# Moving 42 pieces of the two absolute weight sums from the attention groups into the first three projection blocks of a transformer layer

## The chip, the cores and the metric

The kernel runs on all eight cores of one Trainium2 chip. Each core takes one batch element (2048 tokens of width 2048) and reads the same weights; there is no exchange between cores. The metric is the device time in microseconds of the slowest core. The program names the engines PE (TensorE, matmul), DVE (VectorE), ACT (ScalarE), POOL (GpSimd) and SP (SyncE, which here only issues transfers). Each engine takes its instructions strictly in the order written and stops at the first one whose wait isn't met.

## The reference

One layer in two halves, each with a layer norm ahead and a residual add behind:

```
h   = layernorm(x)
q,k,v = h @ W* + h @ A* @ B*            # 16 query heads, 4 key/value heads of 128, rank 16
q,k = rmsnorm, rotary on 64 of 128, q *= gain
y   = causal softmax(q k^T / sqrt(128)) @ v
y  -= (y . v/|v|) v/|v|                 # component along the token's own value removed
x   = x + y @ Wproj + y @ p_A @ p_B
h   = layernorm(x)
s_w = mean(|W|) + 1e-8;  W_q = clip(round(W / s_w), -1, 1) * s_w    # for W_up, W_gate, W_down
x   = x + (silu(h @ W_up^T) * (h @ W_gate^T)) @ W_down^T
```

W_up and W_gate have 8192 x 2048 elements each. A mean of absolute values over all of W_up and one over all of W_gate must be known before the first panel of either is rounded to -1, 0 or 1. This case is about where those two sums are computed. They are the only reason for which the first half of the kernel reads W_up and W_gate at all.

## The kernel before

**Front.** The tokens are 16 row tiles of 128. A first stage (0 to about 173 us) normalises and transposes them into `slabA` and does query, key and value of head group 0. Then `attention` walks four groups, one per key/value head, of 136 score steps each (`PER`; a step is one query tile against one key tile for four heads). A step issues one score matmul (L769), an exponential on ACT (L781), up to two products with the values (L797, four matmuls each), and in the first three groups a share of the next group's query, key and value matmuls (L396, 512 in a group, from step 8 on). DVE and ACT also carry the norms and evictions of those tiles (L436 to L517 on DVE, L416 to L450 on ACT), and POOL the rotary part and two of the steps that finish an output tile. The order is written out by the loop itself: short queues of closures with due steps (`for_act`, `for_dve`, `for_bank`), no scheduler. The program holds attention twice, with and without a shift of the scores, and branches on the size of the gains; all gains are one, so the version without runs. At the start of the fourth group POOL issues sixteen loads that bring Wproj into `slabA`.

**The pieces.** `pieces` cuts W_up and W_gate into 256 pieces of 128 x 1024 float32 (512 KB). `abs_load` has SP load the next piece into one of three places (`pw`), once the place is free; `abs_sum` waits for the piece, sums its absolute values into one column of `pacc` on ACT (L199) or DVE (L202), and at once asks for the next load into the place that came free. So three pieces at most are under way. 13 are summed in the first stage. In the groups the loop keeps a target, `ABS_A` (222) pieces by the end of the third group and 256 by the end of the fourth, and issues a sum when it is behind: one on ACT when ACT has nothing due and the lag is over 1, and one on DVE when DVE has nothing due or the lag is over 3. Steps 0 to 9 of the first three groups issue none. That gives 69, 69 and 70 pieces in the first three groups and 35 in the fourth, 162 of the 256 on DVE.

**Projection.** Four blocks of 512 tokens. A block first multiplies the block's attention output `yts[s % 2]` (2 MB, read back from memory by `load_y`) with the rank-16 matrix (`lowrank_y`, L1154), which is the first thing in a block to need that operand, and then with 16 slices of Wproj (`proj_mm`, L1170 and L1175). `proj_post` adds each slice to the residual on DVE (L1186), squares it on ACT (L1196), and accumulates sum and sum of squares on POOL (L1205, L1208). After three slices of the next block come the statistics and the normalisation of the block (`stats`, `apply`) into `slabB`. The two buffers `yts` take turns: the operand of block s + 1 is loaded at the start of block s, when block s - 1 has been read. `finish_scale` turns the columns of `pacc` into the two scales; it makes DVE wait for everything that ACT has been given so far, and stands behind slice 8 of block 0. The scales are first used in block 3.

**FFN.** 192 panels of up, gate and down, bounded by PE, to the end. Nothing of it is touched.

Of the kernel before, what the change touches and what calls it, by code (L numbers as in the profile page):

```python
# [99 lines left out]
def build_program():  # L100
# [31 lines left out]
    with ExitStack() as outer:  # L132
# [5 lines left out]
        def emit(general):  # L138
# [5 lines left out]
                        "xs0", "xs1", "pw0", "pw1", "pw2", "gns", "ys0", "ys1",  # L144
# [34 lines left out]
            piece_next = [0]  # L179
# [3 lines left out]
            def abs_load(s, slots, sems, frees):  # L183

                n = piece_next[0]
                if n >= len(pieces):
                    return
                piece_next[0] += 1
                mi, src, col = pieces[n]
                wait("sync", frees[s])  # L190
                ld = dma("sync", sems[s], slots[s], src)
                pend.append((slots[s], col, ld, s))
# [419 lines left out]
            pw_args = (pw, ("pw0", "pw1", "pw2"), pw_free)  # L612
            ABS_0 = NT - 3
# [59 lines left out]
            ABS_A = 222  # L673
# [6 lines left out]
            def attention(general):  # L680
# [306 lines left out]
                while n < NPAIR or n_av < NPAIR:  # L987
# [37 lines left out]
                    if n < NPAIR and not (r < 10 and g < HKV - 1):  # L1025

                        lag = (ABS_0 + n * (ABS_A - ABS_0) // (3 * PER) if g < HKV - 1 else
                               ABS_A + (r + 1) * (256 - ABS_A) // PER) - n_abs
# [26 lines left out]
                assert not for_act and not for_pool and piece_next[0] == 256  # L1055
# [95 lines left out]
            def lowrank_y(s):  # L1151
                wait("tensor", pab, yl_tok[s], ya_bank_free[0], front_bank[0])
                for k in range(ND):
                    tp = op("tensor", lambda e, k=k: e.matmul(  # L1154
                        bank(0)[0:48, :], pa[:, k, :], yts[s % 2][:, k, :],
                        start=(k == 0), stop=(k == ND - 1)), inc=(k == ND - 1))
                wait("scalar", tp, blk_end[s - 1] if s else None)
                ya_tok[0] = ya_bank_free[0] = op("scalar", lambda e: e.activation(
                    ya, bank(0)[0:48, :], AF.Copy))
# [265 lines left out]
            load_y(1)  # L1425
            early = []
            for s in range(NB):
                if 1 <= s < NB - 1:
                    load_y(s + 1)
                lowrank_y(s)  # L1430
                if s == 0:
# [11 lines left out]
                    for i in range(5):  # L1443
                        proj_post(s, i)
                else:
# [21 lines left out]
                    proj_post(s, 5)  # L1467
                for i in range(5 if s == 0 else 6, ND):
                    proj_mm(s, i)
                    proj_post(s, i)  # L1470
                    if s == 0 and i == 8:
# [141 lines left out]
```

How the kernel before makes its waits and increments, by code:

```python
    def wait(self, eng, *tokens):  # L46
        for tok in tokens:
            if tok is None:
                continue
            sem, tgt = tok
            assert 0 < tgt <= self.cnt[sem]
            if self.met.get((eng, sem), 0) >= tgt:
                continue
            self.met[eng, sem] = tgt
            h = self.h[sem]
            self.ops[eng].append(lambda e, h=h, tgt=tgt: e.wait_ge(h, tgt))
# [1 line left out]
    def op(self, eng, fn, sem=None, inc=True):  # L58
        if not inc:
            self.ops[eng].append(fn)
            return None
        sem = sem or MAIN[eng]
        h = self.h[sem]
        self.cnt[sem] += 1
        self.ops[eng].append(lambda e, fn=fn, h=h: fn(e).then_inc(h, 1))
        return sem, self.cnt[sem]
# [1474 lines left out]
            def body(e):  # L1541
                for f in fast[eng][:f0[eng]]:
                    f(e)
                if eng in ("tensor", "vector"):
                    e.wait_ge(sems["dv"], flag_set[1])
                    large = e.value_load(flag)
                    with e.If(large == 1):
                        for f in full[eng][g0[eng]:g1[eng]]:
                            f(e)
                    with e.Else():
                        for f in fast[eng][f0[eng]:f1[eng]]:
                            f(e)
                else:
                    for f in fast[eng][f0[eng]:f1[eng]]:
                        f(e)
                for f in fast[eng][f1[eng]:]:
                    f(e)
```

## Time and profile before

| | us |
|---|---|
| Median of three runs (lowest 3891.25, highest 4554.52) | 3892.86 |
| The profiled execution | 3895.69 |
| Its span on the slowest core, core 7 (the cores: 3872.2 to 3894.1) | 3894.1 |
| First stage, to the first steps of attention | about 0 to 173 |
| Attention group 1, 2, 3 (borders by the loads that POOL issues at their starts) | 186 to 382, 382 to 581, 581 to 780 |
| Attention group 4 | 780 to 918 |
| Projection | 918 to about 1230 |
| FFN | about 1230 to 3894 |
| Busy over the span: PE, DVE, ACT, POOL | 3694.9 (95%), 1773.2 (46%), 930.3 (24%), 687.7 (18%) |

The table is read together with the stretches. The shares over the span are dominated by the FFN, in which PE is busy all the time, so 95% says little about the first 1230 us. In the groups PE is at nine tenths, DVE and ACT at two thirds, and the mean busy share of the 16 DMA engines at seven to eight tenths. Matmul ends are modelled, so PE's busy time is an upper value.

### The profile page before, as it was taken

The page shows a single profiled execution, that of the slowest core. Times are in us where ns is not written, and L with a number is a line of the kernel's source. Part 1 is how long each engine was busy: PE and PEld are TensorE (multiplying, and loading weights), DVE is VectorE, ACT ScalarE, POOL GpSimd, SP SyncE. Part 2 cuts the span into 40 slices and gives each one's busy share as a digit, 9 for nine tenths or more (in the row PEclk, how much of TensorE's full clock was granted, in tenths as well). Part 3 has the DMA queues.
Part 4 walks back from the last instruction along what each step waited for, and adds up shares of the span by engine and source line. Part 5 has one row for each costly group of instructions (what it writes and reads, how often), then busy time and mean ns, then how long its engine had stood idle before and what let it go on. Part 6 is the DMA issues. An engine that isn't in the chain of part 4 may idle for free.

```text
span 3894.1 us, 52465 instructions; the slowest of 8 cores (3872.2 to 3894.1 us)
## 1 busy us (share of the span) xinstructions
PE 3694.9 (95%) x19512; PEld 1787.0 (46%) x19512; DVE 1773.2 (46%) x2309; ACT 930.3 (24%) x1662; POOL 687.7 (18%) x835
## 2 busy tenths in 40 slices
PE   6898898958998999999999999999999999999999
PEld 4555555534333444444444444444444444444444
DVE  5666676644346333344433334433333443333443
ACT  4566676754111544200000100000100000101000
POOL 3355555445534000000000000000000000000000
PEclk9999999979999999999999999999999999999999
DMA  6577777696334877546422225632222663222364
GB/s 170 159 217 207 204 218 202 200 206 216 126 116 143 302 276 256 191 177 230 173 76 76 76 76 206 227 141 76 76 76 76 230 230 114 78 76 79 110 229 155
DMA packets 123949, 629.65 MB, mean 162 GB/s; under 512 B 13120, under 2 KB 13440, under 8 KB 73008
## 3 DMA queue, kind: packets, MB, share of 16 engines
q1 hardware_dynamic: 96960, 469.80, 35.6%
q0 software_dynamic: 26736, 156.45, 13.1%
q8 instruction: 163, 2.67, 0.3%
q14 instruction: 90, 0.74, 0.1%
HBM read 555.55 MB, written 92.27 MB: 166 GB/s over the span
## 4 chain that ended last, share of the span: by engine, by line
PE 82%; DMA 7%; DVE 5%; issue 3%; POOL 2%; ACT 1%; DVEq 0%; SPq 0%; POOLq 0%; ACTq 0%
PE accps L1366 67%; PE gps L396 5%; PE accps L1170 4%; DMA pw<-W_gate 3%; PE yps L797 2%; PE sps L769 1%; DMA pw<-W_up 1%; DMA yst<-xb 1%; DMA bm0t<-v_B 1%; DVE pacc L202 1%; DVE slabB L1249 1%; POOL xreg L1208 1%; PE gps L401 1%; DVE ss L436 1%; DMA bm1t<-v_B 0%
## 5 line engine op out<-in xcount | busy, mean ns | idle before, releaser
L1366 PE MATMUL accps<-slabB,xreg 128*128 128x512 bf16 x8192 | 1773.5, 380 | 4.4 <-DVE slabB L1249 4.4
L1366 PEld LDWEIGHTS accps<-slabB,xreg 128*128 128x128 bf16 x8192 | 802.4, 98 | 975.0 <-issue 11.7
L1366 PE MATMUL accps<-slabA,xreg 128*128 128x512 bf16 x4096 | 884.7, 380 | 0.0
L1379 ACT ACTIVATE xreg<-accps,scl 128x512 f32<-128x512 f32 x256 | 175.1, 687 | 2052.4 <-PE accps L1366 2052.4
L1366 PEld LDWEIGHTS accps<-slabA,xreg 128*128 128x128 bf16 x4096 | 400.7, 98 | 483.3
L1334 DVE TENSOR_SCALAR xreg<-xreg,scl 128x2048 bf16<-128x2048 f32 x192 | 247.3, 1288 | 601.9 <-PE accps L1366 577.6
L1337 DVE SCALAR_TENSOR_TENSOR xreg<-xreg,scl 128x2048 bf16<-128x2048 f32 x192 | 453.1, 2360 | 20.4 <-DVE xreg L1334 0.5
L396 PE MATMUL gps<-wq,slabA 128*128 128x512 bf16 (+1 forms) x2048 | 416.9, 335 | 14.8 <-DMA wq<-Wqkv 12.0
L1393 DVE SCALAR_TENSOR_TENSOR xreg<-accps,scl,xreg 128x512 f32<-128x512 f32 x256 | 192.0, 750 | 471.3 <-PE accps L1366 471.3
L1383 DVE TENSOR_TENSOR slabA<-xreg,accps 128x512 bf16<-128x512 f32 x256 | 175.2, 686 | 503.6 <-PE accps L1366 500.4
L781 ACT ACTIVATE pring<-sps 128x512 bf16<-128x512 f32 x510 | 297.7, 610 | 148.6 <-PE sps L769 116.7
L72 POOL DMA_DIRECT2D acc_scr<-xreg x48 | 35.5, 739 | 1558.4 <-DVE xreg L1393 1558.4
L396 PEld LDWEIGHTS gps<-wq,slabA 128*128 128x128 bf16 x2048 | 195.2, 100 | 142.2 <-issue 38.8
L202 DVE TENSOR_REDUCE pacc<-pw 128x1 f32<-128x1024 f32 x162 | 194.3, 1213 | 136.2 <-DMA pw<-W_gate 72.2
L1170 PE MATMUL accps<-xreg,slabA 128*128 128x512 bf16 x1024 | 238.0, 387 | 12.0 <-DVE xreg L1186 8.1
L769 PE MATMUL sps<-qT,kT 128*128 128x512 bf16 x510 | 202.8, 400 | 10.7 <-DVE mq L460 5.6
L1170 PEld LDWEIGHTS accps<-xreg,slabA 128*128 128x128 bf16 x1024 | 97.0, 99 | 138.0 <-issue 35.6
L1420 ACT ACTIVATE xreg<-xreg 128x2048 f32<-128x2048 f32 x64 | 121.8, 1905 | 70.0 <-DMA xreg<-W_down 70.0
L72 POOL DMA_DIRECT2D outT<-xreg x16 | 11.0, 685 | 641.4 <-DVE xreg L1393 641.4
L797 PE MATMUL yps<-v1b,pring 128*128 128x129 bf16 x884 | 88.3, 233 | 32.8 <-DVE t1a L824 23.7
L797 PE MATMUL yps<-v1a,pring 128*128 128x129 bf16 x1088 | 100.9, 227 | 14.6 <-DVE t1b L824 7.4
L797 PEld LDWEIGHTS yps<-v1a,pring 128*128 128x128 bf16 x1088 | 80.0, 101 | 55.2 <-issue 22.9
(165 smaller groups left out, 2165.9 us busy)
## 6 DMA issues: line engine op xcount, KB each, us to landing
xreg<-W_down SPq DMA_DIRECT2D x128, 1024.0 KB, 7.8
pw<-W_up SPq DMA_DIRECT2D x128, 512.0 KB, 5.7
pw<-W_gate SPq DMA_DIRECT2D x128, 512.0 KB, 5.7
xreg<-W_up SPq DMA_DIRECT2D x64, 1024.0 KB, 5.1
xreg<-W_gate SPq DMA_DIRECT2D x64, 1024.0 KB, 5.0
xreg<-acc_scr POOLq DMA_DIRECT2D x64, 1024.0 KB, 7.5
acc_scr<-xreg POOLq DMA_DIRECT2D x48, 1024.0 KB, 5.2
outT<-xreg POOLq DMA_DIRECT2D x16, 1024.0 KB, 5.2
```

The costliest lines, as they stand in the source:

```text
L202: frees[s] = op("vector", lambda e: e.tensor_reduce(pacc[:, col:col + 1], buf, AX.X, ALU.add, apply_absolute_value=True))
L396: op("tensor", lambda e, out=out, dt=dt, w=w, lo=lo, hi=hi: e.matmul(out, slabA[:, dt, ts], w[:, dt % 2, lo:hi], start=(dt == 0), stop=Fal ...
L769: s_tok[n] = op("tensor", lambda e: e.matmul(bank, kT[g % 2][:, kt * 128:(kt + 1) * 128], qT[:, qt, :], start=not general and not first, s ...
L781: a = op("scalar", lambda e: e.activation(p, rbank(bank_of[n]), AF.Exp))
L797: tp = op("tensor", lambda e, h=h: e.matmul(Yv[y][:, h // 2, h % 2, :], p[:, h * 128:(h + 1) * 128], v1[g % 2][:, kt, :], start=first and ...
L1170: op("tensor", lambda e, k=k: e.matmul(bk, wpj[:, i, k, :], yts[s % 2][:, k, :], start=(k == 0), stop=False), inc=False)
L1334: m = op("vector", lambda e: e.tensor_scalar(t, src, scl[:, 8 + mi:9 + mi], None, ALU.is_lt))
L1337: quant_tok[k] = op("vector", lambda e: e.scalar_tensor_tensor(t, src, scl[:, 4 + mi:5 + mi], t, ALU.is_gt, ALU.subtract))
L1366: pan_tok[k][tc] = op("tensor", lambda e, tc=tc, dt=dt, mov=mov: e.matmul(bank(st_ + tc), tern[s][:, dt * 128:(dt + 1) * 128], mov, start= ...
L1379: evict[k][tc] = op("scalar", lambda e, tc=tc, cs=cs: e.activation(silu[:, cs], bank(st_ + tc), AF.Silu, scale=scl[:, 1:2]))
L1383: evict[k][tc] = op("vector", lambda e, tc=tc, cs=cs: e.tensor_tensor(hid[:, j, cs], silu[:, cs], bank(st_ + tc), ALU.mult))
L1393: e.scalar_tensor_tensor(accs[a][:, ds], bank(st_ + tc), scl[:, 12:13], accs[a][:, ds], ALU.mult, ALU.add))
```

## The change

Forty-two pieces are no longer summed in attention. The targets become `ABS_A` = 174 and `ABS_F` = 214, so the groups take 53, 53, 54 and 41 pieces where they took 69, 69, 70 and 35: sixteen fewer in each of the first three, six more in the fourth. The other 42 are summed in blocks 0, 1 and 2 of the projection, 14 in each, all on ACT (`block_pieces`). Their four places lie in the buffer `yts[(s + 1) % 2]`, where the next block's operand will stand. Therefore the load of that operand is issued only behind slice 10 of the block, and waits there for the last of the 14 sums. The first four piece loads of block 0 follow the loads of the residual; those of blocks 1 and 2 follow the load of the next block's residual. `finish_scale` moves from slice 8 of block 0 to slice 14 of block 2.

```diff
-                        "xs0", "xs1", "pw0", "pw1", "pw2", "gns", "ys0", "ys1",
+                        "xs0", "xs1", "pw0", "pw1", "pw2", "gns", "pw3", "ys0", "ys1",
...
-                if n >= len(pieces):
+                if n >= piece_end[0]:
                     return
...
+            ABS_A, ABS_F = 174, 214
+            piece_end[0] = ABS_F
...
-            ABS_A = 222
...
                         lag = (ABS_0 + n * (ABS_A - ABS_0) // (3 * PER) if g < HKV - 1 else
-                               ABS_A + (r + 1) * (256 - ABS_A) // PER) - n_abs
+                               ABS_A + (r + 1) * (ABS_F - ABS_A) // PER) - n_abs
...
             load_x(0, 0)
-            load_y(1)
+            def piece_args(s):
+                return ([xf(16 * ((s + 1) % 2) + 4 * i, 1024) for i in range(4)],
+                        ("pw0", "pw1", "pw2", "pw3"), piece_free)
+
+            piece_free = [None] * 4
+
+            def block_pieces(s, i):
+                args = piece_args(s)
+                if i == 0:
+                    piece_end[0] = ABS_F + 14 * (s + 1)
+                    piece_free[:] = [blk_end[s - 1]] * 4 if s else [None] * 4
+                    if s == 0:
+                        wait("sync", *front_early)
+                    for k in range(4):
+                        abs_load(k, *args)
+                for _ in range(2):
+                    if i >= 2 and pend:
+                        abs_sum("scalar", *args)
+                if i == 10:
+                    assert not pend
+                    wait("sync", *piece_free)
+                    load_y(s + 1)
...
             for s in range(NB):
-                if 1 <= s < NB - 1:
-                    load_y(s + 1)
                 lowrank_y(s)
...
                     for i in range(5):
                         proj_post(s, i)
+                        block_pieces(s, i)
...
                     proj_post(s, 4)
                     proj_post(s, 5)
+                    if s < NB - 1:
+                        for i in range(6):
+                            block_pieces(s, i)
                 for i in range(5 if s == 0 else 6, ND):
                     proj_mm(s, i)
                     proj_post(s, i)
-                    if s == 0 and i == 8:
+                    if s < NB - 1:
+                        block_pieces(s, i)
+                    if s == NB - 2 and i == 14:
                         up_s = finish_scale(1, 64, 128, bank(0))
                         gate_s = finish_scale(2, 192, 128, bank(0))
```

Two places in the order of instructions show the change. The first is ACT in the second attention group, from one square of the queries (L416) to the next; `pring<-sps` are the exponentials, `pw,pacc<-pw` is the sum of a piece. Before:

```order
L416 ACTIVATE sq<-gps 128x512
L781 ACTIVATE pring<-sps 128x512 x2
L426 ACTIVATE sq<-gps 128x256
L429 ACTIVATE vf<-gps 128x128
L781 ACTIVATE pring<-sps 128x512 x2
L447 ACTIVATE lss<-ss,epsc 128x5
L450 ACTIVATE lss<-lss 128x5
L781 ACTIVATE pring<-sps 128x512
L199 ACTIVATE pw,pacc<-pw 128x1024
L781 ACTIVATE pring<-sps 128x512 x3
```

The same stretch of ACT in the changed kernel:

```order
L416 ACTIVATE sq<-gps 128x512
L782 ACTIVATE pring<-sps 128x512 x2
L426 ACTIVATE sq<-gps 128x256
L429 ACTIVATE vf<-gps 128x128
L782 ACTIVATE pring<-sps 128x512 x2
L447 ACTIVATE lss<-ss,epsc 128x5
L450 ACTIVATE lss<-lss 128x5
L782 ACTIVATE pring<-sps 128x512 x4
```

The piece between the exponentials is gone, and nothing else has moved. The second place is SP's queue in block 1 of the projection, from the residual loads of block 1 (`xT`) on; `acc_scr` are the stores of the new residual, `y_scr` is the next block's operand. Before, where the operand's load stands ahead of all of them:

```order
L72 DMA xreg<-y_scr 128x8192 [waits pe]
L72 DMA xreg<-xT 128x4x512 [waits dv,xo0,ac,po]
L72 DMA xreg<-xT 128x4x512 [waits dv,xo1,ac,po]
L72 DMA xreg<-xT 128x4x512 [waits dv,xo2,ac,po]
L72 DMA acc_scr<-slabB 128x4x512 [waits dv]
L72 DMA xreg<-xT 128x4x512 [waits dv,xo3,ac,po]
L72 DMA acc_scr<-xreg 128x4x512 [waits dv] x3
```

And in the changed kernel:

```order
L72 DMA xreg<-xT 128x4x512 [waits dv,xo0,po]
L72 DMA xreg<-xT 128x4x512 [waits dv,xo1,po]
L72 DMA xreg<-xT 128x4x512 [waits dv,xo2,ac,po]
L72 DMA acc_scr<-slabB 128x4x512 [waits dv]
L72 DMA xreg<-xT 128x4x512 [waits dv,xo3,ac,po]
L72 DMA xreg<-W_gate 128x1024 [waits pe]
L72 DMA xreg<-W_gate 128x1024 x3
L72 DMA xreg<-W_gate 128x1024 [waits ac] x10
L72 DMA acc_scr<-xreg 128x4x512 [waits dv]
L72 DMA xreg<-y_scr 128x8192 [waits ac]
```

The operand's load now stands behind fourteen piece loads, ten of which wait for a sum on ACT, and behind one store.

## Rows read from the trace of the kernel before

**Rows 1.** busy time by window, core 7: groups one, two and four (columns in the first line)

```profile
core 7: us, PE busy (x) PEld busy (x) DVE busy (x) ACT busy (x) POOL busy (x), PEclk, DMA share, GB/s
186.00:382.00 196.00, 177.02 (x1377) 106.97 (x1376) 132.40 (x259) 131.79 (x280) 102.70 (x131) 0.95 0.76 213
382.00:581.00 199.00, 176.04 (x1383) 107.50 (x1382) 136.98 (x267) 133.33 (x286) 109.05 (x140) 0.96 0.77 210
780.00:918.00 138.00, 87.48 (x803) 59.79 (x800) 78.19 (x113) 81.22 (x160) 68.87 (x71) 0.80 0.90 225
```

**Rows 2.** waits of the first, second and third group: us in total, times, longest

```profile
DVE pacc L202 <- DMA pw<-W_up: 38.0, 16, 6.4
...
DVE pacc L202 <- DMA pw<-W_up: 25.6, 13, 5.0
...
DVE pacc L202 <- DMA pw<-W_gate: 28.0, 16, 3.3
```

**Rows 3.** instructions on tile pw, whole span: count, ns min/median/max, first and last start

```profile
L202 DVE TENSOR_REDUCE pacc<-pw x162: 1202/1212/1221, 196.8 to 916.4; 128x1 f32<-128x1024 f32 x162
L199 ACT ACTIVATE pw<-pw x94: 1046/1050/1078, 80.1 to 785.7; 128x1024 f32<-128x1024 f32 x94
...
DMA to landing us min/median/max: 3.6/5.7/20.0
```

**Rows 4.** timeline, second group: start us, us, engine, line, what, idle before and releaser

```profile
456.46 1.22 DVE L202 TENSOR_REDUCE pacc<-pw 128x1 f32<-128x1024 f32 x1 [5.03 <-DMA pw<-W_up]
...
462.58 1.05 ACT L199 ACTIVATE pw<-pw 128x1024 f32<-128x1024 f32 x1
...
463.10 0.62 PE L797 MATMUL yps<-v1b,pring 128*128 128x129 bf16 x8 [1.28 <-DVE t1a L824]
```

**Rows 5.** windows of 20 us, instructions of L396 (query, key, value matmuls) alone

```profile
486.00:506.00 20.00, 13.06 (x66) 6.00 (x65) 1.00 0.81 217
586.00:606.00 20.00, 6.39 (x29) 2.83 (x29) 0.91 0.76 170
```

**Rows 6.** last group in two parts, instructions of L202 alone

```profile
780.00:861.00 81.00, 14.86 (x13) 0.72 1.01 213
861.00:918.00 57.00, 26.56 (x22) 0.92 0.76 242
```

**Rows 7.** DMA issues in the same two parts: count, KB each, median us to landing

```profile
pw<-W_gate SPq DMA_DIRECT2D x14, 512.0 KB, 12.5
...
pw<-W_gate SPq DMA_DIRECT2D x19, 512.0 KB, 5.8
```

**Rows 8.** DMA in 1030 to 1045, in 40 slices of 1039 to 1068, in 1060 to 1080

```profile
DMA packets 2096, 4.18 MB, mean 278 GB/s; under 512 B 57, under 2 KB 57, under 8 KB 2096
...
GB/s 407 410 412 387 322 342 302 376 395 407 249 164 62 37 25 0 0 0 0 0 263 407 410 364 3 0 0 0 0 0 0 0 0 0 11 0 0 0 0 0
...
xreg<-y_scr SPq DMA_DIRECT2D x1, 2048.0 KB, 9.2
```

**Rows 9.** timeline of projection block 1

```profile
1039.36 0.37 SPq L72 DMA_DIRECT2D xreg<-xT  x1
...
1045.17 0.63 ACT L1196 ACTIVATE xreg<-xreg 128x512 f32<-128x512 f32 x1 [2.00 <-POOL xreg L1208]
...
1064.55 0.63 ACT L1196 ACTIVATE xreg<-xreg 128x512 f32<-128x512 f32 x1 [2.93 <-DVE xreg L1186]
...
1067.40 3.63 PE L1154 MATMUL accps<-xreg,pa 128*48 128x512 bf16 x16
```

**Rows 10.** timeline of projection block 0

```profile
945.04 3.55 SPq L72 DMA_DIRECT2D xreg<-xT  x3
...
962.66 0.35 PE L1260 MATMUL accps<-tots,ones_f 128*128 128x1 f32 x2 [3.11 <-DVE tots L1257]
964.56 6.28 PE L1170 MATMUL accps<-xreg,slabA 128*128 128x512 bf16 x16
...
994.34 3.63 PE L1154 MATMUL accps<-xreg,pa 128*48 128x512 bf16 x16
```

More of the change, by code:

```diff
@@ L178, in emit @@
                       for k in range(64) for h in range(2)]
-            piece_next = [0]
+            piece_next, piece_end = [0], [0]
             pend = []
@@ L1054, in attention @@
                     abs_sum("vector", *pw_args)
-                assert not for_act and not for_pool and piece_next[0] == 256
+                assert not for_act and not for_pool and piece_next[0] == ABS_F
                 while next_slot:
@@ L1151, in lowrank_y @@
             def lowrank_y(s):
-                wait("tensor", pab, yl_tok[s], ya_bank_free[0], front_bank[0])
+                wait("tensor", pab, yl_tok[s], *ya_bank_free, front_bank[0])
                 for k in range(ND):
```

## The prediction

> **What bounds the kernel now.** I read the busy time by stretch first. In the first and second group PE is busy for 177 of 196 us and for 176 of 199 us, at a mean granted clock of 0.95 and 0.96; DVE and ACT are busy for two thirds [rows 1]. So PE has some 20 us of holes in a group and loses some more to the lower of its two clock levels after them. In the fourth group it is busy for 87 of 138 us, and the DMA engines at 0.90 [rows 1]. Next the waits. DVE, which takes its work in order, stands before a piece sum for its DMA 16, 13 and 16 times in the three groups, for 38.0, 25.6 and 28.0 us [rows 2]. The timeline shows what that does: DVE stands 5.03 us until 456.46, its late work ends late, and PE stands at 463.10 for 1.28 us, released by a DVE instruction behind the sum [rows 4]. Stepping through the three groups in this way, nearly every hole of PE outside the first 15 us of a group follows a piece wait within 7 us.
>
> Why pieces are late is arithmetic. A load lands in a median of 5.7 us, a sum on DVE takes 1.21 us [rows 3], and there are three places: a place turns over in about 7 us. A score step takes 1.44 us (196 us / 136). Where the third piece after a given one comes fewer than five steps later, it has to be waited for. Counting through the loop's order, that is so 64 times in the first three groups.
>
> **Change, part 1: sixteen pieces fewer in each of three groups.** The same count in the changed order gives 14 instead of 64. What a group could take: where nothing is held up, 66 of the L396 matmuls pass in 20 us [rows 5]; 512 in a group make 155 us, and the eight steps without them some 7, so 162. The group takes 196 to 199, so 35 us are lost. About half of that is lost at the group's start, where short output tiles follow each other and only 29 matmuls pass in 20 us [rows 5] with few pieces there; removing pieces hardly changes that. The other 18 us I put on the piece waits: about 12 of standing and 6 of lower clock. With 78% (50 of 64) of the causes gone, 14 us a group, **-42 us** in all. The removed sums themselves (1.21 us on DVE, 1.05 on ACT [rows 3]) lie beside PE's work and I count nothing more for them. Bounds: at least -20, if only half of the standing goes and the clock does not recover; at most -60, if the starts improve too. I take a value near the middle since rows 4 ties the standing to the pieces directly.
>
> **Part 2: six pieces more in the last group.** It falls in two. Until 861 us the DMA engines are full (1.01) with Wproj and 13 pieces [rows 6]; two more pieces of 0.52 MB at 213 GB/s are 5 us. After it, 22 pieces pass in 57 us [rows 6], one in 2.6; landing takes 5.8 us [rows 7], and three places allow one in (5.8 + 1.2)/3 = 2.3 us, so this part is already nearly as fast as its three places let it be. Four more are 4 x 1.2 (DVE only) to 4 x 2.6 us; I take 7. Together **+12**, between 0 (ACT and DMA absorb all) and +20. In the first part a piece takes 12.5 us to land [rows 7]; if a further piece costs a whole turn of its place, 12.5/3 = 4.2 us, two cost 8 instead of 5, and part 2 becomes +15. The Trainium skill, "DMA: Bandwidth & Descriptors", section "Queues, rings and completion order", says that a DMA engine serves the queues that have work in turn, packet by packet; by that rule three places on SP's queue against sixteen Wproj loads on POOL's get a fixed share and the +15 holds. The trace (12.5 us against 5.8) leans that way; it moves the sum by 3 us and I leave it at the bytes.
>
> **Part 3: the next operand arrives late.** This is where the change costs. Block 1: the residual load of block 2 is issued at 1039.36, and the low-rank matmuls of block 2, which need the operand, start at 1067.40, directly behind the last slice [rows 9]. In these 28 us now come, in one chain, that load (1 MB), 14 pieces (7.3 MB), the last sum, then a store (1 MB) and the operand (2.1 MB). The engines moved 278 GB/s over 15 busy us and 302 to 412 in single slices of 0.7 us [rows 8]. At 350 GB/s a piece takes 1.5 us: the residual has landed at about 1044.4, the fourteenth piece at 1065.4, its sum ends at 1066.7, and the operand, 9.2 us from issue to landing [rows 8], lands at 1076. PE stands **8 to 9 us**, and the sixteen matmuls behind a stand take longer: after the holes at 962 to 964 us they took 6.28 us [rows 10], against 3.63 in the even run of rows 9. I add 2 us for the clock, so +11.
>
> Block 0: the residual loads start at 945.04 [rows 10], four of 1 MB; the pieces come behind them, the first at about 960.5, the last, with a store between, at 983; sum, operand at 993.5. The low-rank matmuls of block 1 began at 994.34 [rows 10]. Without `finish_scale` at slice 8, which held PE for 3.1 us at 962.66 and about 1.1 behind it and cost 2.6 in clock [rows 10], they could begin 7 us sooner; the operand takes that back, and with its own clock loss block 0 is at **+1**.
>
> Block 2: `finish_scale` stands behind slice 14, and its wait is for all of ACT. In block 1, eight pieces on ACT stand ahead of the square of slice 6 and six more ahead of that of slice 9. ACT is held by the pieces until about 1066.7, and from there the squares follow POOL at 2.63 us each (0.63 busy and 2.00 of waiting [rows 9]). The square of slice 14, at 1064.55 now [rows 9], comes at about 1077. In block 2's time that is a stand of 13 us for PE, then 2 to 3 for the two small reductions, then slice 15 (3.9 us); the operand has long landed. The low-rank matmuls of block 3 begin 16 us late, with the clock **+18**.
>
> Projection: 1 + 11 + 18 = **+30**. Bounds: at 400 GB/s it is -2 + 8 + 14 = +20, at 278 GB/s +9 + 19 + 23 = +51; if PE did not wait at all it would be -7. I take 350, which lies between the mean over 15 us and the slices.
>
> **Sum.** -42 + 12 + 30 = 0 against the profiled execution of 3895.7 us, which lies 2.8 above the median of the runs, 3892.9. I add 2 us for parts that I may have counted at nothing, and forecast **3895 us**; each time below is 3892.9 + 2 and the sum of its case. It is no change that a measurement of this kernel can tell. It can tell about 2%, that is 78 us.
>
> **Rivals.** *The projection takes the pieces for nothing.* For it: of the 40 slices of rows 8 more than half are at or near 0 GB/s, so the engines have room. Against it: 11.4 MB in 28 us, less the fixed part of two landings and a sum, needs well over the 412 GB/s of the best slice [rows 8]. Then -42 + 12 - 7 = -37, **3858 us**; chance 0.18.
>
> *The groups don't speed up: another wait takes the pieces' place.* The holes of PE end at DVE or POOL work, and DVE keeps two thirds of its load; POOL is busy for 103 to 109 of 196 us [rows 1] and its chain of three steps for an output tile sets the pace at a group's start. If it does elsewhere too, a group gains 5 us: -15 + 12 + 30 = +27, **3922 us**, slower than before. It decides if PE's holes stay at 15 us or more in a group while the piece waits fall below 10. For it: the 29 matmuls in 20 us [rows 5]. Against it: the stretch of 66 between. Chance 0.18.
>
> *Memory is slower with all cores in the projection reading pieces*, at 278 GB/s: -42 + 12 + 51 = +21, 3916 us; chance 0.14.
>
> *The groups gain all they can* (-60) at the forecast's projection: 3877 us; chance 0.12. The forecast itself has 0.35 within some 10 us; 0.03 is left for what I have not seen.
>
> **The numbers.** The range takes in all of these: from 3858 up, a little further down where the first and fourth would add up in part, gives low 3858; the two slow cases with some overlap give high 3928. Faster by over 2% would need -78 us, more than the groups' whole loss outside their starts: 0.01. Slower by over 2% needs the highest bound of each term at once: 0.02. Same: 0.97.
>
> **What would show it.** In the changed profile: groups one to three of 182 to 186 us, with DVE's wait for pieces under 10 us each; group four of about 150 us; PE standing before the low-rank matmuls of blocks 1 and 2 for some 6 and 9 us, released by the operand's load; a stand of about 13 us at the first reduction of `finish_scale` in block 2; the FFN unchanged. The forecast is wrong if the operand lands before PE asks for it, or if the groups stay at 190 us or more.

## The result and the profile after

The changed kernel is **slower by 0.8%**: the ratio of its time to the time before is 1.008, with a 95% interval of 1.0051 to 1.0109. That is clear of the noise and below the 2% that counts as a change. Two of its runs took 3923.3 and 3926.2 us; the profiled one is the first of these, and its slowest core, core 2, has a span of 3921.8 us, 27.7 above that of before, which was core 7's. (In some executions one half of the chip ran at a lower clock: they are left out of all comparisons, where a median holds them I give the lowest run, and of the profiled execution of x10_spread the other half is read.) Forecast were 3895 us with a range of 3858 to 3928.

The span splits into stages. The borders are POOL's bias and Wproj loads at the start of a group, the first low-rank matmul of a projection block, and the statistics of block 3's end. "Block 0" is so the time from the low-rank matmuls of block 0 to those of block 1.

| us | groups 1, 2, 3 | group 4 | blocks 0, 1, 2 | block 3 | FFN | span |
|---|---|---|---|---|---|---|
| before | 196.3, 199.3, 199.8 | 135.8 | 75.7, 73.1, 72.6 | 82.8 | 2671.2 | 3894.1 |
| after | 186.1, 182.6, 183.3 | 153.0 | 82.5, 91.4, 101.1 | 82.6 | 2671.5 | 3921.8 |
| difference | -43.4 | +17.2 | +6.8, +18.3, +28.5 | -0.2 | +0.3 | +27.7 |

The three groups gained what was forecast (-42). The last group lost 17 instead of 12, and the projection 54 instead of 30. That leaves +27.

This table compares the slowest core of each execution, and these are two different cores. The same borders on all eight cores, as means with the lowest and highest core, give:

| us | groups 1 to 3 together | group 4 | blocks 0 to 2 together | span |
|---|---|---|---|---|
| before | 585.5 (579.6 to 595.5) | 138.5 (135.6 to 142.1) | 220.1 (218.5 to 221.4) | 3883.8 |
| after | 549.4 (545.2 to 553.3) | 148.8 (146.5 to 153.0) | 274.2 (268.6 to 276.7) | 3912.4 |
| difference | -36.1 | +10.3 | +54.1 | +28.6 |

So core 7 of before has the longest three groups and nearly the shortest last one, and core 2 of after the longest last one. Some 7 us of the -43.4 and as many of the +17.2 belong to these two cores and not to the change; they cancel in the sum.

First the groups, busy time by window of the changed kernel, as [rows 1] for before (the fourth line is the last group):

```profile
core 2: us, PE busy (x) PEld busy (x) DVE busy (x) ACT busy (x) POOL busy (x), PEclk, DMA share, GB/s
189.00:374.00 185.00, 173.25 (x1378) 105.73 (x1376) 124.96 (x255) 126.36 (x266) 101.84 (x130) 0.97 0.67 182
374.00:557.00 183.00, 171.17 (x1384) 105.64 (x1384) 130.09 (x263) 125.93 (x268) 109.82 (x141) 0.98 0.63 183
557.00:740.00 183.00, 170.63 (x1377) 105.66 (x1378) 126.16 (x252) 125.24 (x265) 104.68 (x131) 0.97 0.60 174
740.00:893.00 153.00, 87.02 (x759) 59.31 (x757) 83.24 (x115) 79.21 (x152) 68.12 (x69) 0.78 0.86 217
```

And DVE's waits for pieces in the first, second and third group, to be held against [rows 2] (us in total, times, longest; the last two lines are both of the third group, whose pieces come from both matrices):

```profile
DVE pacc L202 <- DMA pw<-W_up: 17.2, 7, 4.9
...
DVE pacc L202 <- DMA pw<-W_up: 11.4, 6, 3.3
...
DVE pacc L202 <- DMA pw<-W_gate: 7.4, 2, 4.5
DVE pacc L202 <- DMA pw<-W_up: 3.9, 2, 2.8
```

In the second group of before, the last pieces are already of W_gate, and their waits are a line of their own that [rows 2] does not have:

```profile
DVE pacc L202 <- DMA pw<-W_gate: 6.5, 3, 4.5
```

PE's work is the same; its holes in the second group shrank from 23 to 12 us, and 5 us of its busy time went with the clock (0.96 to 0.98). The waits for pieces fell there from 25.6 + 6.5 = 32.1 us to 11.4, and to 17.2 and 11.3 us in the other two; the forecast had all three under 10.

The last group, cut as [rows 6] cuts it, DVE's piece sums alone, and the landing of the pieces in both parts (count, KB, median us), as [rows 7]:

```profile
740.00:821.00 81.00, 15.69 (x13) 0.75 0.98 207
821.00:893.00 72.00, 32.65 (x28) 0.81 0.73 227
```

```profile
pw<-W_gate SPq DMA_DIRECT2D x13, 512.0 KB, 12.5
...
pw<-W_gate SPq DMA_DIRECT2D x25, 512.0 KB, 5.5
```

On this core nothing about the pieces moved in the first 81 us: 13 sums and 12.5 us to land, as before. Behind it 28 pieces take 72 us, one in 2.57 us, nearly the pace at which 22 took 57 us (2.59) [rows 6]. At that pace the six more are 15 us. Counted from each group's own start, the eight cores sum 15.1 pieces on average in their first 81 us, against 13.9 before, so the other cores do take some of the six there.

Now the projection: where PE stands, from its timeline (start us, us, ..., idle before and what released it):

```profile
975.14 5.46 PE L1155 MATMUL accps<-xreg,pa 128*48 128x512 bf16 x16 [14.04 <-DMA xreg<-y_scr]
...
1066.54 5.83 PE L1155 MATMUL accps<-xreg,pa 128*48 128x512 bf16 x16 [16.81 <-DMA xreg<-y_scr]
...
1158.96 0.56 PE L1261 MATMUL accps<-tots,ones_f 128*128 128x1 f32 x2 [21.39 <-DVE tots L1258]
```

Three stands of 14.0, 16.8 and 21.4 us; before there was none over 2.3 us in blocks 1 and 2, and one of 3.1 in block 0 [rows 10]. They stand where the forecast put them and have the releasers that it named, but it gave them 6, 9 and 13 us. The windows of the three blocks show the clock that followed (PEclk is the third value from the right, 0.83 in block 2):

```profile
893.00:975.00 82.00, 68.10 (x300) 27.90 (x298) 11.79 (x18) 25.73 (x46) 32.88 (x28) 0.92 0.66 217
975.00:1067.00 92.00, 71.55 (x294) 28.66 (x295) 31.55 (x49) 27.77 (x48) 37.98 (x31) 0.89 0.63 197
1067.00:1168.00 101.00, 75.04 (x298) 30.23 (x297) 32.34 (x57) 28.20 (x49) 42.84 (x35) 0.83 0.57 182
```

Blocks 1 and 2 before, in the same columns:

```profile
994.00:1067.00 73.00, 69.13 (x293) 27.92 (x292) 31.58 (x49) 12.48 (x20) 35.64 (x30) 0.98 0.41 144
1067.00:1140.00 73.00, 69.55 (x294) 28.06 (x293) 31.58 (x49) 12.47 (x20) 37.41 (x31) 0.98 0.41 144
```

And SP's queue in block 1, whose issues before are in [rows 8] and [rows 9] (start us, us from the first to the last of the issues, count), with ACT's first and last sum and the first step of POOL behind the eight sums:

```profile
1021.61 0.37 SPq L72 DMA_DIRECT2D xreg<-xT  x1
1022.08 28.36 SPq L72 DMA_DIRECT2D xreg<-W_gate  x14
...
1057.72 0.33 SPq L72 DMA_DIRECT2D xreg<-y_scr  x1
```

```profile
1032.90 1.06 ACT L199 ACTIVATE xreg<-xreg 128x1024 f32<-128x1024 f32 x1 [9.54 <-DMA xreg<-W_gate]
...
1056.49 1.06 ACT L199 ACTIVATE xreg<-xreg 128x1024 f32<-128x1024 f32 x1 [0.68 <-DMA xreg<-W_gate]
```

```profile
1047.63 1.27 POOL L1209 TENSOR_TENSOR xreg<-xreg 128x512 f32<-128x512 f32 x1 [18.91 <-ACT xreg L1197]
```

From the residual's load (1021.61) to the operand's (1057.72) pass 36.1 us, where the forecast had 27.3. The first sum comes 11.3 us after the residual's issue instead of 6.5, and the other thirteen follow at 1.81 us each (23.59 us from first to last), not 1.5. A piece of 0.52 MB in 1.81 us is 290 GB/s, and that is what the DMA engines show in these 37 us:

```profile
DMA packets 3671, 10.64 MB, mean 288 GB/s; under 512 B 284, under 2 KB 284, under 8 KB 3667
## 3 DMA queue, kind: packets, MB, share of 16 engines
q1 hardware_dynamic: 3667, 10.60, 92.3%
```

They are busy at 0.92, so by that share more places than four could have added some 9% at most: the batch goes at about the rate that the engines sustain. In block 0 the stretch of the fourteen loads (922 to 958 us) had 312 GB/s at 0.93, in block 2 (1112 to 1150) 295 at 0.91. And while ACT works off the eight sums ahead of the square of slice 6, POOL stands 18.9 us.

### The profile page after: what moved, and what is told of

Read it like the earlier page. It is cut to its first block, busy times and chain, and to the rows that moved or that the text cites. A ratio compares the mean times of both kernels' runs of the same rounds, so it can differ in the third digit from the quotient of the medians.

```text
span 3921.8 us, 52472 instructions; the slowest of 8 cores (3903.4 to 3921.8 us)
## 1 busy us (share of the span) xinstructions
PE 3688.7 (94%) x19512; PEld 1785.3 (46%) x19512; DVE 1754.7 (45%) x2295; ACT 954.0 (24%) x1690; POOL 687.6 (18%) x835
## 4 chain that ended last, share of the span: by engine, by line
PE 80%; DMA 8%; DVE 5%; issue 3%; POOL 2%; ACT 1%; SPq 0%; DVEq 0%; POOLq 0%; ACTq 0%
PE accps L1367 67%; PE gps L396 6%; DMA pw<-W_gate 3%; DMA xreg<-W_gate 2%; PE yps L798 2%; PE sps L770 2%; PE accps L1171 1%; DMA wq<-Wqkv 1%; DVE slabB L1250 1%; DMA yst<-xb 1%; DVE pacc L202 1%; DVE slabB L1248 1%; PE gps L401 1%; POOL xreg L1209 1%; PE accps L1155 1%
## 5 line engine op out<-in xcount | busy, mean ns | idle before, releaser
L1367 PEld LDWEIGHTS accps<-slabB,xreg 128*128 128x128 bf16 x8192 | 802.4, 98 | 974.8 <-issue 11.5
L396 PE MATMUL gps<-wq,slabA 128*128 128x512 bf16 (+1 forms) x2048 | 411.0, 331 | 18.3 <-DMA wq<-Wqkv 13.7
L782 ACT ACTIVATE pring<-sps 128x512 bf16<-128x512 f32 x510 | 299.4, 605 | 182.6 <-PE sps L770 147.6
L396 PEld LDWEIGHTS gps<-wq,slabA 128*128 128x128 bf16 x2048 | 192.8, 99 | 142.6 <-issue 39.5
L202 DVE TENSOR_REDUCE pacc<-pw 128x1 f32<-128x1024 f32 x148 | 176.2, 1211 | 90.7 <-DMA pw<-W_gate 58.0
L72 POOL DMA_DIRECT2D xreg<-acc_scr x64 | 33.9, 529 | 384.0 <-ACT xreg L1421 380.8
```

The source lines that it names most:

```text
L202: frees[s] = op("vector", lambda e: e.tensor_reduce(pacc[:, col:col + 1], buf, AX.X, ALU.add, apply_absolute_value=True))
L396: op("tensor", lambda e, out=out, dt=dt, w=w, lo=lo, hi=hi: e.matmul(out, slabA[:, dt, ts], w[:, dt % 2, lo:hi], start=(dt == 0), stop=Fal ...
L782: a = op("scalar", lambda e: e.activation(p, rbank(bank_of[n]), AF.Exp))
L1367: pan_tok[k][tc] = op("tensor", lambda e, tc=tc, dt=dt, mov=mov: e.matmul(bank(st_ + tc), tern[s][:, dt * 128:(dt + 1) * 128], mov, start= ...
```

## The experiments

All of them are read by stages (sum of the blocks 0 to 2: before 221.4, after 275.0 us):

| us | groups 1, 2, 3 | group 4 | blocks 0, 1, 2 | block 3 | span |
|---|---|---|---|---|---|
| x1_scale_wait | 186.1, 184.4, 183.5 | 149.5 | 84.0, 90.2, 89.1 | 82.9 | 3907.8 |
| x2_own_places | 186.3, 183.2, 183.1 | 145.5 | 68.5, 90.2, 117.7 | 82.6 | 3917.7 |
| x3_both | 185.6, 184.5, 183.5 | 151.6 | 67.8, 89.6, 106.3 | 82.6 | 3910.4 |
| x4_groups_alone | 187.2, 187.1, 184.4 | 148.7 | 74.2, 72.7, 72.6 | 82.6 | 3870.5 |
| x6_short_loads | 182.0, 181.4, 179.6 | 111.8 | 75.1, 72.9, 72.6 | 82.6 | 3851.5 |
| x7_short_sums | 184.4, 188.5, 187.5 | 132.5 | 73.4, 72.9, 72.6 | 82.6 | 3856.6 |
| x8_quarter_loads | 183.2, 183.2, 185.1 | 145.6 | 74.1, 84.8, 93.6 | 82.6 | 3897.0 |
| x9_copy_on_dve | 185.5, 187.3, 184.9 | 146.9 | 68.1, 85.1, 104.6 | 82.6 | 3902.6 |
| x10_spread | 183.4, 184.0, 185.0 | 153.2 | 67.7, 72.3, 72.2 | 85.1 | 3863.1 |
| x11_spread18 | 184.0, 183.6, 184.9 | 126.9 | 69.1, 77.6, 72.6 | 85.3 | 3841.7 |

x6's slowest core took 2706 us for the FFN, 35 more than the others, so its span is not compared. For x10 core 4 is read.

**x4_groups_alone: the groups without the projection.** The loads and sums of the 42 pieces are left out (W_gate's mean is taken over the 86 that remain), the operand is loaded early and `finish_scale` is back at slice 8:

```diff
-                for _ in range(2):
+                for _ in range(0):
...
+                if 1 <= s < NB - 1:
+                    load_y(s + 1)
...
-                    if s == NB - 2 and i == 14:
+                    if s == 0 and i == 8:
```

> The change in the groups alone: 214 pieces in the groups as in the changed kernel, none in the projection (42 pieces of W_gate are left out, its mean is taken over the other 86), operand and finish_scale as in the kernel before. Theory: -43 in the first three groups, +17 in the last, 0 in the projection: about 3868 us. Rival (the groups' gain is partly the slowest core's luck, or the projection gains by itself): outside 3858 to 3878.

Ratio to before 0.9927 (0.9877 to 0.9976), lowest run 3865.4. The groups gain 36.7 and the last loses 12.9, while the blocks are as before within 1.5 us. On the means of the eight cores it is -33.1 and +9.6. So the two parts of the change are independent: it has a gain of about 24 us in attention, by either reading, and everything else is the projection's.

**x1_scale_wait: only the wait of `finish_scale` is narrowed.** It waits for the last piece's sum and no longer for all that ACT has been given:

```diff
-            def finish_scale(mi, lo, n, bk):
-                wait("vector", ctx.now("ac"))
+            def finish_scale(mi, lo, n, bk, last=None):
+                wait("vector", ctx.now("ac") if last is None else last)
```

> finish_scale in block 2 waits only for the last piece sum and not for all that ACT has been given. Theory (the 21 us stand of PE at the first reduction is the wait for the squares that stand behind the pieces): the stand falls to 1 to 3 us, but PE then stands before the low-rank matmuls of block 3, because the operand lands only 19 us after slice 14; 9 to 11 us less than the changed kernel, about 3914 us. Rival (PE stands for something else in block 2): less than 3 us less, 3922 us or more.

Ratio 1.0059 (1.0036 to 1.0082), lowest run 3909.3. Block 2 gains 12.0 us, the others nothing:

```profile
1065.84 4.98 PE L1155 MATMUL accps<-xreg,pa 128*48 128x512 bf16 x16 [15.37 <-DMA xreg<-y_scr]
1146.16 0.56 PE L1261 MATMUL accps<-tots,ones_f 128*128 128x1 f32 x2 [10.18 <-DVE tots L1258]
```

The stand at `finish_scale` falls from 21.4 to 10.2 us and does not vanish: it now waits for the fourteenth sum itself, which is late too. The wait for all of ACT was half of the stand. The stand before block 3's low-rank matmuls that was expected in its place did not come: the operand had landed at 1154.35, and they start at 1154.92 without a wait.

**x2_own_places: the operand is not delayed.** The pieces get places in a slice of `slabB` that is free then, and the next operand is loaded at the head of the block, as before:

```diff
+            load_y(1)
+            spare = slabB_h[:, 2 * 8192:3 * 8192].bitcast(F32)
...
-                return ([xf(16 * ((s + 1) % 2) + 4 * i, 1024) for i in range(4)],
+                return ([spare[:, i * 1024:(i + 1) * 1024] for i in range(4)],
...
-                    wait("sync", *piece_free)
-                    load_y(s + 1)
+                if 1 <= s < NB - 1:
+                    load_y(s + 1)
```

> The four places of the projection's pieces lie in slice 2 of slabB, which nothing uses before block 3, and the next operand is loaded as early as in the kernel before. Theory (the operand is late because it shares the places): no stand before the low-rank matmuls of blocks 1 and 2, block 2 still stands some 20 us at finish_scale; about 32 to 36 us less than the changed kernel, 3889 us. Rival (the pieces' transfers and their sums on ACT slow the blocks wherever they lie): blocks 0 and 1 stay above 80 us each, 3910 us or more.

Lowest run 3919.2. The three blocks together take 276.4 us, against 275.0: **nothing gained**, where 32 to 36 us were expected (270.7 against 274.2 on the means of the eight cores). PE starts the low-rank matmuls on time and stands one instruction later:

```profile
977.68 0.58 PE L1176 MATMUL accps<-ya,pb 16*128 16x512 bf16 x1 [14.76 <-ACT ya L1159]
...
1070.74 0.58 PE L1176 MATMUL accps<-ya,pb 16*128 16x512 bf16 x1 [17.66 <-ACT ya L1159]
...
1155.93 0.56 PE L1261 MATMUL accps<-tots,ones_f 128*128 128x1 f32 x2 [21.31 <-DVE tots L1258]
```

It needs `ya`, which ACT copies out of the accumulator. ACT takes its work in order, and ahead of that copy stand squares that wait for POOL. A second chain ran beside the operand's, hidden by it and as long. (The stand is now behind the border of the block, so block 0 seems to gain 14 us and block 2 to lose 17.)

**x3_both: x1 and x2 together.**

> Own places for the pieces, operand early, and finish_scale waiting only for the last piece. Theory: the projection is as long as in the kernel before (-7 in block 0, +4 in block 2), the groups keep their -43 and the last group its +17: 3862 to 3870 us. Rival (contention of 22 MB of pieces with the residual loads and stores): 10 us or more above the run without any pieces in the projection.

Lowest run 3911.9; blocks together 263.7, against 263.3 in x1. With the narrower wait, too, it makes little difference whether the operand is early (259.6 and 264.4 on the means of the eight cores). The stands are 14.3, 15.2 and 11.5 us.

**x9_copy_on_dve: x3, and `ya` is copied by DVE**, which takes the copy out of ACT's queue:

```diff
-                ya_tok[0] = ya_bank_free[0] = op("scalar", lambda e: e.activation(
-                    ya, bank(0)[0:48, :], AF.Copy))
+                ya_tok[0] = ya_bank_free[0] = op("vector", lambda e: e.tensor_copy(
+                    ya, bank(0)[0:48, :]))
```

> As the run with own places and the last-piece wait, and the eviction of the low-rank product (ya) goes from ACT to DVE. Theory (with the operand early PE stands some 15 us in blocks 1 and 2 for that eviction, since it stands in ACT's queue behind the squares, which stand behind the pieces and then follow POOL at 2.63 us each): those two stands go, a smaller one of 4 to 7 us comes up before the statistics, which need POOL's last sum; 15 to 22 us less than with ACT, about 3893 us. Rival (the stands are the transfers' doing): no change, 3908 us or more.

Lowest run 3898.5; blocks together 257.8, some 6 us less than x3 (8 on the means of the eight cores), where 15 to 22 were expected. In blocks 0 and 1 neither the operand nor `ya` is waited for any more, and PE stands at a third place, the statistics, which need POOL's last output (at `finish_scale` it still stands 11.7 us). The second fence is POOL in block 1:

```profile
987.40 2.05 PE L1229 MATMUL accps<-xreg,jm_f 128*128 128x512 f32 x2 [10.63 <-POOL xreg L1209]
...
1075.82 2.04 PE L1229 MATMUL accps<-xreg,jm_f 128*128 128x512 f32 x2 [13.94 <-POOL xreg L1209]
```

```profile
1044.99 1.27 POOL L1209 TENSOR_TENSOR xreg<-xreg 128x512 f32<-128x512 f32 x1 [19.30 <-ACT xreg L1197]
```

This names what is common to all of them. The square of slice 6 stands behind eight sums on ACT, which come as the pieces land; POOL stands 19 us for it, and 3.4 and 1.9 us more behind the six sums that follow. Only then does it work without a pause, at 2.63 us a slice against PE's 3.9, so it gets back 1.3 us a slice, in too few slices: when the block ends it is 11 to 14 us late, and whatever PE asks for there is late.

**x8_quarter_loads: are the bytes to blame?** The changed kernel with ten of the fourteen loads of a block cut to a quarter of their columns (0.13 MB, with W_gate's mean taken over the 86 whole pieces); order, sums and waits stay:

```diff
-                ld = dma("sync", sems[s], slots[s], src)
+                w = 1024 if n < ABS_F or (n - ABS_F) % 14 < 4 else 256
+                ld = dma("sync", sems[s], slots[s][:, 0:w], src[:, 0:w])
```

> The changed kernel, in whose projection ten of a block's 14 pieces are loaded for 256 of 1024 columns, all sums as long as before (the 42 pieces are left out of the mean of W_gate). Theory (the projection's extra time over the forecast is the transfer rate, 288 GB/s for 350): PE stands 0 to 3 us for the operand in block 1 and 3 to 8 in block 2, and 10 to 15 at finish_scale, 3885 to 3898 us. Rival (the sums and squares on ACT alone hold the blocks): stands as in the changed kernel, 3910 us or more.

One run, 3898.5 us. The blocks together take 252.5: 22.5 us less than after, 31 more than before. The stands are 5.7, 9.4 and 15.1 us, each above what the theory of the rate had left (0 to 3, 3 to 8 and 10 to 15) and well below the changed kernel's. So with little more than half of the loads' bytes gone, more than half of the loss stays. The bytes are a part of it; the batch in its place, sums and the landing of its first load, is the other (in block 1 of x8 ACT still stands 8.1 us for the first piece, and the fourteen sums then take 17.3 us from first to last start, against 23.6 in the changed kernel).

**x10_spread: same bytes, other order.** x9 with the pieces as a continuous stream. The sums no longer come in a batch of eight, but four in the pass over the output, where ACT has little to do, and one behind each square from slice 6 (from slice 2 in block 0); `finish_scale` goes to slice 8 of block 3:

```diff
-                for _ in range(2):
-                    if i >= 2 and pend:
-                        abs_sum("scalar", *args)
+                if i >= (2 if s == 0 else 6):
+                    one_piece()
...
+                        if i in (1, 5, 9, 13) and s < NB - 1:
+                            one_piece()
...
-                    if s < NB - 1:
-                        for i in range(6):
-                            block_pieces(s, i)
```

> The same 42 pieces, 14 in each of the first three projection blocks, but spread: with places of their own (a slice of slabB), so that the next operand's place is free from the start, one sum on ACT behind each square from slice 2 (block 0), or four in the pass over the output and one behind each square from slice 6 (blocks 1 and 2); ya's copy is on DVE, and finish_scale stands behind slice 8 of block 3 and waits for the last piece alone. Theory (what costs in the blocks is the crowd: fourteen loads ahead of the operand on SP, and eight sums at one go ahead of a square on ACT, behind which POOL's chain of 2.63 us a slice can't catch up): no square waits for more than one sum, PE has no stand over 3 us in the low-rank part, block 0 is 68 to 70 us (finish_scale has left it), blocks 1 and 2 73 to 76, block 3 some 2 to 3 us more than 82.8; groups 182 to 187 and the last 145 to 153 as in the changed kernel; span 3865 to 3880. Rival (what costs is the DMA engines' share: 7.3 MB more in a block land late wherever they stand, and sums on ACT wait for them): blocks 1 and 2 stay at 80 us or more and the span above 3885.

**Ratio to before 0.9916 (0.9896 to 0.9936)**, lowest run 3858.1. The blocks together take 212.2 us, 45.6 less than x9, with the same fourteen loads and sums for each in the program. Two things differ from x9, the order of the sums and the place of `finish_scale`, and the second takes away one of x9's three stands, the one of 11.7 us; the other two, of 10.6 and 13.9 us, are the order's alone. Blocks 1 and 2 of x10 by window, and ACT's waits for its pieces and POOL's for the squares in both blocks together (us in total, times, longest):

```profile
964.00:1037.00 73.00, 68.25 (x296) 27.82 (x296) 32.51 (x51) 32.50 (x58) 45.74 (x37) 1.00 0.91 291
1037.00:1109.00 72.00, 67.32 (x292) 27.45 (x291) 32.01 (x51) 26.51 (x47) 37.27 (x31) 1.00 0.75 240
```

```profile
ACT slabB L199 <- DMA slabB<-W_gate: 8.4, 4, 4.2
```

```profile
POOL xreg L1209 <- ACT xreg L1197: 0.2, 1, 0.2
```

In block 1 the DMA engines are busy at 0.91 and move 291 GB/s, over the whole block, and PE does not notice: clock 1.00, no stand above 2.3 us. (ACT works through the sums later than the program's borders say: 9, 18 and 14 of them fall into the windows of blocks 0, 1 and 2, and 13, 18 and 11 of the loads.) In the changed kernel the same block moved 197 GB/s on average, because the batch moved 288 in 37 us of it and little was asked for in the rest. The profiled span of core 4, 3863.1 us, is just below what the first theory expected, and the rival, late landings wherever the pieces stand, is refuted. Against before, blocks 1 and 2 are no longer than they were (72.3 and 72.2 us), so the pieces cost nothing there. Block 0 gains 8 and block 3 loses 2, since `finish_scale` has gone from one to the other: PE's stands of 2.1 and 1.1 us at its two reductions are now in block 3.

**x11_spread18: 18 pieces a block**, so that the last group has 29 and not 41:

```diff
-            ABS_A, ABS_F = 174, 214
+            ABS_A, ABS_F = 174, 202
...
-                    if i in (() if s == 0 else ()):
+                    if i in ((9, 11, 13, 15) if s == 0 else (9, 12)):
                         one_piece()
...
-                        if i in (1, 5, 9, 13) and s < NB - 1:
+                        if i in (1, 4, 5, 8, 9, 13) and s < NB - 1:
```

> As the spread version, with 18 pieces in each of the three blocks (four more in each: a second sum behind four slices of block 0 and two of blocks 1 and 2, and two more in the pass over the output), so that the last group takes 28 of them and not 40. Theory: the last group, where the DMA engines are the bound, falls by 12 pieces at 1.2 to 2.6 us each as far as they are bound there, 14 to 20 us, to 127 to 135 us; the blocks take 9.4 MB each beside their own 9 MB, some 250 GB/s in 73 us, and lengthen by 0 to 2 us each; span 3845 to 3865. Rival (the blocks are full at 14): each block lengthens by 5 us or more against the spread version, and the span stays within 5 us of it.

**Ratio 0.988 (0.986 to 0.990)**, lowest run 3841.4: this version beats both kernels. The last group falls to 126.9 us, below that of before (135.8) and as the theory expected. Block 1 is where the room ends:

```profile
937.00:1014.00 77.00, 68.45 (x292) 27.85 (x290) 32.17 (x50) 37.59 (x70) 41.22 (x33) 0.98 0.95 292
```

```profile
955.87 2.05 PE L1229 MATMUL accps<-xreg,jm_f 128*128 128x512 f32 x2 [3.87 <-POOL xreg L1209]
```

At 0.95 and 292 GB/s, with 24 piece loads in this window, a stand at the statistics comes back on core 2 (block 1: 77.6 us); core 4 of the same execution has 72.5 there, and the mean of the eight cores is 75.0.

**x6_short_loads and x7_short_sums: why the groups lose time.** Both are the kernel before. In x6 all but the first sixteen pieces are loaded with 64 of their 1024 columns, with whole sums; in x7 the loads are whole and the sums read 64 columns (their mean scaled by 16):

```diff
+                w = 1024 if n < 16 else 64
+                ld = dma("sync", sems[s], slots[s][:, 0:w], src[:, 0:w])
```

```diff
-                        pacc[:, col:col + 1], buf, AX.X, ALU.add, apply_absolute_value=True))
+                        pacc[:, col:col + 1], buf[:, 0:64], AX.X, ALU.add, apply_absolute_value=True))
```

> The kernel before, all 256 pieces where they were and every sum over 1024 columns, but from the seventeenth piece on a load brings only 64 columns; the sums read older weights in the rest. Theory (the groups lose time because pieces land late, not because they are summed): DVE's waits for pieces nearly vanish and each of the first three groups falls to 175 to 185 us, the last to 115 to 125. Rival (the sums' own time on DVE and ACT holds PE): the first three groups stay at 192 us or more.

> The kernel before with full loads, but each sum reads only 64 of 1024 columns (the scale is multiplied by 16). Theory (late landing): places turn over in 6 instead of 7 us, so waits shrink a little and the first three groups take 190 to 195 us. Rival (the sums' own time): 180 to 187 us.

One run each: 3853.0 and 3858.1 us. The three groups gain 52.4 us in x6 and 35.0 in x7 (42.7 and 32.9 on the means of the eight cores). DVE's waits for pieces in the second group, of x6 and then of x7:

```profile
DVE pacc L203 <- DMA pw<-W_up: 4.9, 5, 2.3
```

```profile
DVE pacc L202 <- DMA pw<-W_up: 34.2, 14, 4.8
DVE pacc L202 <- DMA pw<-W_gate: 14.7, 9, 3.6
```

In x7 DVE waits for pieces *longer* than before (34.2 + 14.7 = 48.9 us against 32.1), and the group is still 11 us shorter. So the landings are not the whole cause: the sum's own 1.2 us, which I had counted at nothing, makes DVE late as well, and either half taken away gives most of the gain. How much of it belongs to which stays open, since the two overlap, and a short sum also frees its place for the next load a microsecond sooner. x6 shows one thing more: the last group, with its 35 sums but hardly any of their bytes, takes 111.8 us instead of 135.8.

## Why the prediction was right, and where it was not

**The call was right**: no change of 2% in either direction, and the time lies in the range, near its upper end. The middle was 28 us too low.

**Part 1, the groups: -42 forecast, -43.4 measured**, with groups of 182.6 to 186.1 us as written. That the two agree to a microsecond is in part luck: on the means of the eight cores the groups gained 36.1, and 36.7 in x4. One reason given for it was too narrow: x7 contradicts "I count nothing more for them" of the sums' engine time. DVE's waits for pieces stayed over the 10 us that were forecast (17.2, 11.4 and 11.3), and [rows 2] left out 6.5 us of them in the second group of before. The rival in which another wait takes the pieces' place, with a gain of 5 us a group, is refuted: PE's holes fell to about 12 us in each group, and in x4, where they stayed at 15 to 17 us, the groups still gained 9 to 15.

**Part 2, the last group: +12 forecast, +17.2 measured** (+12.9 in x4, which has the same last group, and +10.3 on the means of the eight cores, so the term was right within what the cores scatter). What erred is its second part, 4 x 1.2 to 4 x 2.6 us, of which I took 7. The pace after is 2.57 us a piece on core 2, as before, which is the upper end; x11 against x10 says much the same, with twelve pieces fewer and 26.3 us less, 2.2 us each (2.0 on the means). In the first part 13 pieces land in 12.5 us in both kernels, while PE does less beside them (309 matmuls instead of 340 in the 81 us from the group's start). By the rule of the Trainium skill, "DMA: Bandwidth & Descriptors", section "Queues, rings and completion order", by which queues with work are served in turn, the term was +15. The 13 pieces in 81 us on core 2 agree with it, but the other seven cores summed 15 or 16 pieces from the group's start, and before none of the eight more than 14, so no run here settles it.

**Part 3, the projection: +30 forecast, +53.6 measured.** This is the term that was mis-sized: the places, the releasers and their order of length were right. Two sizes failed. The first is the rate: I took 350 GB/s, between "the mean over 15 us and the slices"; the batch of block 1 ran at 288. The engines reach 400 GB/s in single slices, and no batch of 10 MB held it (312, 288 and 295 GB/s). The pace is only half of it, though. The operand's load was issued 8.8 us later in its chain than forecast (36.1 for 27.3), and 4.1 of them are the thirteen steps of 1.81 for 1.5 us. The other 4.8 lie ahead of the first sum, where I had 5.0 us for the residual and 1.5 for the first piece. The residual's load alone took 7.9 us to land here, and 7.7 before, which the trace of before had to show (count, KB, us to landing, before and after):

```profile
xreg<-xT SPq DMA_DIRECT2D x1, 1024.0 KB, 7.7
...
xreg<-xT SPq DMA_DIRECT2D x1, 1024.0 KB, 7.9
```

At the 278 GB/s of [rows 8] the text had +9, +19 and +23 = +51; measured were +6.8, +18.3 and +28.5. The rival with slower memory, 3916 us at a chance of 0.14, is nearest to what happened, with some 5 us more in the last group. The terms can be added up from rows: block 0 has 14.0 of standing less the 6.8 of `finish_scale` that went [rows 10], which is 7.2; block 1 has 16.8 and about 2 more for the clock; block 2 has 21.4 and 1.1 at the two reductions, and 5.5 us more of PE's busy time than in the same block before, at a clock of 0.83. My 2 us for the clock there were too few.

**What I did not see** is that there were two chains. I followed the operand's in blocks 0 and 1, and ACT's and POOL's only to `finish_scale`. x2 shows that ACT's alone holds PE as long, through `ya`. Had the operand been free, the forecast by my steps would have been some 17 us lower, and x2 says that next to nothing would have been gained. That the places came out right was luck: of two chains about equally long, I had followed the one that ends last.

**The rival in which the projection takes the pieces for nothing** (0.18) is false for this change and true for x10. Against it stood that 11.4 MB don't go through 28 us. That was right, and 28 us was a property of the order, not of the projection: in block 1 of x10 eighteen pieces, and all else that the block moves, went through its 73 us at 291 GB/s.

## What to carry to other kernels

Room that a profile shows as an average (DMA engines at 0.4 in a block) was had here only by work that is spread over it. As a batch ahead of an in-order engine's next work, the same loads and sums made the four blocks 36 us longer than before (x9), of which 11.7 us is a stand at `finish_scale`, placed too near behind the last sum. One at a time behind that work, and with `finish_scale` out of the way, they left the four blocks 7 us shorter (x10). Price a batch at the rate that the engines hold when they are full, and not at the peaks of their slices, and its first landing at what the trace has for such a load; and before you remove the wait that the profile names, look for the chain that runs beside it, since the profile names only the one that came last. And compare more than the slowest core: here it was another core in each kernel, which moved 7 us from one stage to the next.

## What the runs showed of the hardware

With all eight cores reading, a core's DMA engines moved 312 GB/s at a share of 0.93, 288 at 0.92 and 295 at 0.91 in the three batches of the changed kernel, and 291 at 0.91 and 292 at 0.95 in the streams of x10 and x11, with 512 KB loads and single slices above 400. And the holes of PE were paid twice: in block 2 the same matmuls were busy for 75.0 us at a clock of 0.83, against 67.3 at 1.00 in x10, which is a third of the 21.4 us of standing on top.
